# Sends of GpSimd regrouped from the last batch to the first expert tiles, and one shift moved

## The reference

```python
h = _layernorm(x, axis=-1) * (1 + ca) + sa
x = x + ga * _L0_attn_ref(h, W, b)          # exp(tanh(scores * 1/distance)), rows normalised, times h
h = _layernorm(x, axis=-1) * (1 + cb) + sb
x = x + gb * _L0_ffn_ref(h, ...)            # experts
...
logits = xf @ Wg
top_vals, top_idx = jax.lax.top_k(logits, TOP_K)     # TOP_K = 2
top_w = jax.nn.softmax(top_vals, axis=-1)
h = jax.nn.relu(jnp.einsum('td,edf->tef', xf, W1) + b1)
sparse = jnp.einsum('te,tef,efd->td', combine, h, W2)
shared = jax.nn.relu(xf @ Ws1 + bs1) @ Ws2 + bs2
```

## Time and profile before

| what | us |
|---|---|
| median of 3 runs | 642.19 (642.18 to 644.39) |
| the profiled execution's own time | 641.25 |
| its span, first to last instruction | 639.5 |
| PE busy | 613.3 (96%) |
| DVE busy | 459.0 (72%) |
| ACT busy | 406.3 (64%) |
| POOL busy | 350.3 (55%) |
| 64 sends from `work` (L622), mean of one | 1.027 |

### The profile page before, as it was taken

How to read it: one execution, slowest core, us unless ns; L and a number is a source line. 1 busy time by engine, 2 the same in 40 slices (tenths; PEclk the granted TensorE clock), 3 DMA queues, 4 the chain that set the end, 5 groups by cost and what they waited for, 6 DMA issues and landing times.

```text
span 639.5 us, 13351 instructions
## 1 busy us (share of the span) xinstructions
PE 613.3 (96%) x4339; PEld 557.5 (87%) x4339; DVE 459.0 (72%) x1425; ACT 406.3 (64%) x647; POOL 350.3 (55%) x347
## 2 busy tenths in 40 slices
PE   7899999999999998969999999999999999999997
PEld 5788898788888887858999999999999999998897
DVE  7869798999989896966842676665556544452598
ACT  3698778778787876725565656665555656463551
POOL 5450526867666666665763565566656556466100
PEclk8999999999999999988999999999999999999999
DMA  7500000110111111110752555567666566521793
GB/s 295 196 14 1 2 2 18 34 35 30 34 34 35 34 35 38 39 46 25 243 168 83 180 180 182 184 187 213 182 205 192 183 189 191 177 68 31 268 403 128
DMA packets 30031, 76.46 MB, mean 120 GB/s; under 512 B 7142, under 2 KB 11646, under 8 KB 29856
## 3 DMA queue, kind: packets, MB, share of 16 engines
q1 hardware_dynamic: 20624, 58.49, 28.1%
q0 software_dynamic: 8640, 16.93, 7.9%
q10 hardware_dynamic: 720, 0.47, 0.2%
HBM read 53.53 MB, written 23.24 MB: 120 GB/s over the span
## 4 chain that ended last, share of the span: by engine, by line
PE 60%; DVE 22%; ACT 5%; issue 5%; POOL 3%; another core or an unknown queue 3%; DMA 1%; POOLq 0%; SPq 0%; DVEq 0%; ACTq 0%
PE value L2060 24%; PE score L1840 8%; PE score L1842 8%; PE score L1841 8%; PE value L1868 6%; DVE work L1238 4%; DVE rows_all L1225 2%; DVE stats L1121 2%; PE value L2108 2%; PE misc L1882 2%; ACT work L873 2%; DVE rows_all L1260 2%; ACT work L875 2%; POOL rstd L602 1%
## 5 line engine op out<-in xcount | busy, mean ns | idle before, releaser
L817 POOL DMA_INDIRECT rows_z<-tile_y,tags x138 | 142.4, 1032 | 101.1 <-issue 43.7
L1840 PE MATMUL score<-h_hi,h_lo 128*128 128x512 f32 (+1 forms) x252 | 94.4, 374 | 0.3 <-ACT work L904 0.2
L1868 PE MATMUL value<-w_ring,work 128*128 128x129 f32 x768 | 93.2, 277 | 0.8 <-ACT work L875 0.3
L1868 PEld LDWEIGHTS value<-w_ring,work 128*128 128x128 f32 x768 | 89.8, 192 | 4.7 <-ACT work L875 2.0
L873 ACT ACTIVATE work<-work 128x1024 f32<-128x1024 f32 x64 | 67.3, 1052 | 38.3 <-DVE work L1238 36.2
L1842 PE MATMUL score<-h_hi,h_lo 128*128 128x512 f32 (+1 forms) x252 | 89.4, 355 | 0.0
L904 ACT ACTIVATE work<-score,w_ring 128x512 f32<-128x512 f32 (+1 forms) x96 | 53.2, 617 | 55.7 <-PE score L1842 41.8
L622 POOL DMA_INDIRECT rows_x<-work,slot x64 | 65.7, 1027 | 35.0 <-issue 16.9
L1238 DVE TENSOR_TENSOR work<-score,lw 128x1024 f32<-128x1024 f32 x64 | 76.6, 1215 | 5.0 <-remote 2.3
L1841 PE MATMUL score<-h_hi,h_lo 128*128 128x512 f32 (+1 forms) x220 | 76.4, 347 | 0.0
L2060 PE MATMUL value<-w_ring,work 128*128 128x128 f32 x640 | 75.4, 275 | 0.0
(11 more groups left out here) (282 smaller groups left out, 1208.4 us busy)
## 6 DMA issues: line engine op xcount, KB each, us to landing
w_ring<-packs SPq DMA_DIRECT2D x24, 578.0 KB
rows_all<-packs SPq DMA_DIRECT2D x23, 578.0 KB
lw<-rows_x SPq DMA_DIRECT2D x24, 260.0 KB
res<-x SPq DMA_DIRECT2D x8, 512.0 KB, 6.5
h_t<-rows_z SPq DMA_DIRECT2D x3, 1024.0 KB, 11.7
mod<-mod_rows SPq DMA_DIRECT2D x1, 2560.0 KB, 8.8
rows_z<-tile_y,tags POOLq DMA_INDIRECT x142
rows_all<-rows_z SPq DMA_DIRECT2D x2, 1024.0 KB, 13.2
```

The costliest lines, as they stand in the source:

```text
L817: nc.gpsimd.indirect_dma_start(rows_z[:, :], bass.IndirectOffsetOnAxis(ap=tags[pos][:, k, 0:1].bitcast(I32), axis=0), tile_y[par][:, k, :] ...
L1840: nc.tensor.matmul(out, a_lo, b_hi, start=True, stop=False)
L1868: ins = nc.tensor.matmul(value[:, s // 3, c0:c0 + D + 1], prob[:, t % 4, s * P:(s + 1) * P], normal[b % 3][:, t, :], start=(t == 0 and s % ...
```

## The change

Only GpSimd's program changes. There are three edits.

1. In the last batch each step sends two and not three: the waits on `tanh_done` and the third send of the steps 4 to 7 are gone, so that (5, 0) to (5, 7) are sent in it where it was (5, 0) to (5, 11).
2. The shift of batch 7 moves from batch 6, step 6, to batch 7, ahead of the send of step 3, behind the fourth `score_used`.
3. Behind the last batch 40 sends remain and not 36. The first seven, which had no waits of their own, now stand behind `value_step`, up(0), down(0) and up(1). After `rstd_2(B - 1)` the others come in threes behind up(3), down(1), up(4), down(2), and so on, and the last two groups have two and one.

```diff
                 if t < FIRST:
                     return [(b - 3, 2 * G - LATE + 2 * t + i) for i in range(2)]
-                each = 2 if b < B - 1 else 3
-                return [(b - 2, each * (t - FIRST) + i) for i in range(each)]
+                return [(b - 2, 2 * (t - FIRST) + i) for i in range(2)]
...
                 pool.wait_ge(score_used, G * b + 4)
+                add_shift(b)
                 send_step(b, 3, 0)
                 pool.wait_ge(exp_done, G * b + 4)
                 send_step(b, 3, 1)
-                pool.wait_ge(tanh_done, G * b + 4)
-                send_step(b, 3, 2)
...
                 pool.wait_ge(score_used, G * b + 7)
-                if b == B - 2:
-                    add_shift(b + 1)
                 send_step(b, 6, 0)
...
-            order = iter([(B - 3, m) for m in range(3 * (G - FIRST), 2 * G)] + [(b, m) for b in (B - 2, B - 1) for m in range(2 * G)])
+            order = iter([(B - 3, m) for m in range(2 * (G - FIRST), 2 * G)] + [(b, m) for b in (B - 2, B - 1) for m in range(2 * G)])
...
-            for _ in range(7):
-                send_next()
+            pool.wait_ge(value_step, G * B)
+            send_next()
+            send_next()
+            pool.wait_ge(up_ready, HALVES)
+            send_next()
+            send_next()
+            pool.wait_ge(down_ready, 1)
+            send_next()
+            send_next()
+            pool.wait_ge(up_ready, HALVES * 2)
+            send_next()
             rstd_2(B - 1)
-            pool.wait_ge(up_ready, HALVES * 3)
+            pool.wait_ge(up_ready, HALVES * 4)
+            send_next()
             send_next()
             send_next()
             pool.wait_ge(down_ready, 2)
             send_next()
             send_next()
             send_next()
-            pool.wait_ge(up_ready, HALVES * 4)
+            pool.wait_ge(up_ready, HALVES * 5)
...
+            for n in range(6, FRONT):
+                pool.wait_ge(up_ready, HALVES * (n + 1))
+                send_next()
+                send_next()
+                send_next()
+                pool.wait_ge(down_ready, n - 1)
+                send_next()
+                send_next()
+                send_next()
+            pool.wait_ge(up_ready, HALVES * (FRONT + 1))
+            send_next()
+            send_next()
+            pool.wait_ge(down_ready, FRONT - 1)
+            send_next()
```

More of the change, by code:

```diff
@@ L672, in last_batch @@
                 rstd_2(b - 1)
-                pool.wait_ge(tanh_done, G * b + 5)
-                send_step(b, 4, 2)
                 pool.wait_ge(score_used, G * b + 6)
@@ L678, in last_batch @@
                 send_step(b, 5, 1)
-                pool.wait_ge(tanh_done, G * b + 6)
-                send_step(b, 5, 2)
                 pool.wait_ge(score_used, G * b + 7)
@@ L684, in last_batch @@
                 send_step(b, 6, 1)
-                pool.wait_ge(tanh_done, G * b + 7)
-                send_step(b, 6, 2)
                 pool.wait_ge(score_used, G * b + 8)
@@ L690, in last_batch @@
                 send_step(b, 7, 1)
-                pool.wait_ge(tanh_done, G * b + 8)
-                send_step(b, 7, 2)
             def second_batch(b):
@@ L792, in _ @@
             send_next()
-            pool.wait_ge(up_ready, HALVES * 5)
+            pool.wait_ge(up_ready, HALVES * 6)
             send_next()
             send_next()
-            for n in range(4, FRONT):
-                pool.wait_ge(down_ready, n)
+            send_next()
+            pool.wait_ge(down_ready, 4)
+            send_next()
[3 more added lines that the diff above has]
+                pool.wait_ge(up_ready, HALVES * (n + 1))
                 send_next()
                 send_next()
-                pool.wait_ge(up_ready, HALVES * (n + 2))
+                send_next()
+                pool.wait_ge(down_ready, n - 1)
                 send_next()
                 send_next()
+                send_next()
[4 more added lines that the diff above has]
+            send_next()
             def send(i, pos, paced=True):
```

## The result

The change took 664.39 us (median of 4 runs, 663.33 to 664.73) where the kernel before took 643.29 us in the same rounds (642.18 to 644.64). The ratio is 1.0324, with a 95% interval of 1.0295 to 1.0353: 21.1 us slower, where +3.8 was forecast, and outside the range of 641.7 to 650.5. The profiled execution took 664.24 us with a span of 662.5.

The account below looks back on a forecast made before the run. It took late PE signals behind unbroken runs of GpSimd sends to bound the front. Its terms, -0.5 last batch, 0 front, +1.3 clock and +3.0 tail, summed to +3.8, forecasting 646.0 us, range 641.7 to 650.5.

Parts of the forecast that it names:

- the shift: Last batch: GpSimd's shift beside VectorE's work taken to cost 0, with up to 1 us kept for the range.
- the landing of (5, 15): Behind up(3): the send lands 2.5 us after issue, at 304.1, so `last_rows` starts at about 304.2.
- working rule: GpSimd's sends: five or more without a pause hold PE's signals until about 1 us after, or pass them about 3 us late.
- rival A: Front: the late signals are PE's own and remain, so the change takes 649.2 us; chance 0.13.
- Last batch: Two sends a step and the moved shift: from 1.8 us gained to 1.3 lost, taken as -0.5.
- Front, first half: Attention to up(3): with prompt signals down(0) follows right behind up(0), and up(3) ends 5.4 us earlier.
- The wait that takes its place: `last_rows` waits for (5, 15), so the front's 5.4 us become idle time before `ranks(7)`, at 312.2 to 312.8.
- The clock: PE before up(4): 5.4 us of idle time lowers the granted clock, costing +1.3 us, from 0 to 1.7.
- Tail: From up(4) on: 27 sends without a pause make signals and tile 4's rows late, +3.0 us, from +1 to +5.7.
- B: Rival: the tail does no harm, a busy PE hiding all lateness, so the change takes 643.5 us; chance 0.26.
- C: Rival: faster, the last batch's gain carrying to `ranks(7)` with clock up and tail hidden, 638.9 us; chance 0.11.

Follow-up runs that it names:

- e9: The kernel before without the waits on `up_ready` and `down_ready` behind `rstd_2(7)`: 667.52 against 642.29 us, ratio 1.0387.
- e10: e9 with a 1.67 us power operation on GpSimd, its output unread, behind each three sends: 643.94 us, ratio 1.0037 to the kernel before.
- e7: e1 with (5, 15) sent first behind `rstd_2(7)`, that group waiting for up(3), not up(2): 649.47 us, ratio 1.0093 to the kernel before.
- e1: The kernel before with its first seven sends behind the waits of the change: 632.68 against 632.59 us, ratio 0.9996.
- e4: The change with the shift of batch 7 back in batch 6: 646.45 us against 632.59 us for the kernel before, ratio 1.0212.
- e5: The change again, unedited, on a chip that holds signals: 664.12 us, ratio 1.0336 to the kernel before.
- e6: The kernel before with the shift of batch 7 moved from batch 6 to batch 7: 643.55 against 642.44 us, ratio 1.0018.
- e3: The change with (5, 15) sent ahead of `rstd_2(7)`: 639.93 us against 632.59 us for the kernel before, ratio 1.0102.
- e11: The change with (5, 15) ahead of `rstd_2(7)` and the shift in batch 6: 651.90 us against 642.29 us for the kernel before, ratio 1.0126.

## Why the prediction was wrong, point by point

Three terms of the sum failed: the shift, taken at 0, cost 2.1 us; the landing of (5, 15), taken at 2.5 us, took 6.15, so that `ranks(7)` did not stay where it was; and the tail, taken at +3.0, cost 14.6. The tail is the largest.

**What bounds the kernel, and the working rule.** Right in kind. Runs of sends hold back PE's completion signals; e9 against e10 shows it, and rival A (the late signals are PE's own) falls: the front gained 6.95 us. "Until about 1 us after the run" is what e9 did (312.10 to 313.08); in the change's last run it was 3.5 us (361.38 to 364.89). They are not PE's signals alone: in e7's run of eleven VectorE's are late by 2 us. And the run that I read as nine sends from 274.10 on has no longer gap than 0.31 us from 266.67 on, 14 sends, with prompt signals in its first ten us. What I did not know is that it belongs to the chip: on one of the chips the same kernels show none of it. The Trainium skill's page "Perfetto Trace Analysis", against which I weighed the rule, has a semaphore update pushed when PSUM acknowledges the write. The traces of e1 to e4 agree, with no late signal. In the others waiters see it up to 12.7 us behind the modelled end of the matmul; whether it is pushed late or comes through late is not shown.

**Last batch.** Forecast -0.5 (bounds -1.8 and +1.3), measured +2.1, outside. The failed step is "I take 0" for the shift. I had looked only at L1260. The instruction that met the shift was another one, 128x8 in size, and it was held for all of it. The Trainium skill's page "GPSIMD Engine Reference" (specifications) names contention with VectorE's instructions in a 2-port mode or with two SBUF inputs, and I had looked for the second kind alone. The traces agree that VectorE can be held (3.02 and 3.01 us instead of 0.17), but the instruction has one input, and no row shows its mode. The run of eight made the logits of batch 5 2.1 us late, within the 1.4 to 4.5 of the text, but whether that cost anything beside the shift is not shown: they stand together in the change, e5 and e6, and the loss is no larger than e3's against e4, which have no late signal (2.7 us). Two sends a step gained 0.3 us (e11) of the 1.8 that the text allowed for.

**Front, first half.** Right: forecast -5.4, measured -6.95, and -5.6 in e5; the 1.4 us between them is the clock of up(0), which I had left low. down(0) stands right behind up(0) (286.38 behind 286.24).

**The wait that takes its place.** Right in mechanism, too small by 3.4 us. The 2.5 us from the issue of the last send to SyncE's load are rows from a stage with idle DMA queues. At 302 us SyncE starts three loads of 578 KB, and the send landed 6 us behind its issue. `ranks(7)` came at 317.66 where 312.2 to 312.8 was forecast. The loads stood in the trace of before, from 302.65 on. That they make the send late is likely and not shown. I priced a transfer by its kind and not by what is in the queues with it.

**The clock.** Right in mechanism: +2.6 where 1.3 was taken. PEclk is 0.50 from 318 to 323, nearly all of up(4), behind an idle time of 9.05 us where 5.4 was forecast; that the longer idle time is what kept the clock down longer was not tested.

**Tail.** The largest miss: +14.6 where +3.0 was taken and +5.7 was the end of the range. The text let each pair of tiles grow at most to the length of its six sends, 7.6 us, as though lateness were the same for each run. For the first pairs that was near: up to the first expert's up (last matmul at 341.45 before, 351.25 in the change) only 1.9 us are lost. The other 12.7 go behind it, in the run of 15 sends and after. The longest lateness grows with the run (2 to 5 us behind six sends, 4 behind nine in the kernel before, 9 behind 13 and 13 behind 16 in e9, 11 behind 15 in the change), and in the runs of 15 and 16 PE itself stops. No late signal that I had read stood behind more than nine sends, so that the range had no row for 15, and it should have been left open upwards. POOL's run of "27 sends without a pause" was in fact cut into 6, 6 and 15 behind the first six. The first cut, 1.73 us, is its own wait on a late signal; the second, 3.11 us, stands where e3 and e4 pause for 2.0 us with no signal late.

**Rivals.** B (the tail does no harm) is what the chip without held signals does, but for tile 4's rows. C and A are out.

## What to carry to other kernels

Leave room in the price of a transfer for what is in the queues at its place, and price a held-back signal by the length of the run that holds it. If a wait for a far producer is moved behind new work, every consumer of the old order needs its new time: one send moved past one wait cost 9 to 10 us here. On a chip that holds signals, a pause of 1.7 us behind each third indirect DMA was enough to remove 24 of 25 us, and it needs no wait on another engine.

## What the runs showed of the hardware

- In unbroken runs of GpSimd's indirect DMAs (1.27 us apart), completion signals of PE come late by 2 to 5 us behind six, 9 us behind 13, 11 us behind 15 and 13 us behind 16 of them, and in the last two runs PE issues only a matmul or two every 0.7 to 2.1 us. VectorE's signals were 2 us late in a run of eleven; one of ScalarE's was on time in the run of 15. Two of the three chips of the experiments do this and one does not. The kernel before takes 642.4 and 632.6 us on them; how much of the 10 us is late signals was not separated. Why, and what in the DMAs does it (their descriptors or their writes), stays open. So does what counts as a pause: in the kernel before, sends follow each other from 266.67 on as well, some of them 1.4 us long, and no signal is late before 277.
- A one-input 128x8 operation of VectorE (0.17 us elsewhere) that met a tensor operation of GpSimd (128x1024, two inputs, 2.37 us) took 3.02 us and ended with it, on the chips of both kinds. It had started 0.6 us ahead of it.
- A send that took 2.5 us from issue to the waiter with empty queues took 5.6 to 6.2 us behind 1.7 MB of loads, on the chips of both kinds (e7, the change, e4). That the loads do it was not tested by moving them.
